# Attention over eight batches, with the loop on the engines written out as straight code

## The reference, cut to what matters

```python
x: (8, 512, 128) float32;  H = 16 heads of DH = 64
mod = silu(c) @ wmod                      # six rows per batch: sa, ca, ga, sb, cb, gb
h = layernorm(x) * (1 + ca) + sa
q, k, v = h @ Wq.T, h @ Wk.T, h @ Wv.T    # per head
q, k = l2norm(q) * q_scale, l2norm(k) * k_scale
attn = softmax(q @ k.T * DH ** -0.5)
x = x + ga * ((attn @ v) @ Wo.T + bo)
h = layernorm(x) * (1 + cb) + sb
x = x + gb * (shared_ffn(h) + top2_of_8_experts(h))   # experts with a capacity limit
```

## Time and profile before

| what | value |
|---|---|
| median of 3 runs | 1329.26 us (1327.91 to 1329.69) |
| profiled execution, its own time | 1331.88 us |
| its span, first to last instruction | 1330.0 us |
| mean granted TensorE clock | 0.967 |
| TensorE matmul busy | 1244.9 us, 94% of the span |
| VectorE, ScalarE, GpSimd busy | 988.1, 972.8, 849.6 us |
| attention batches 1 to 6 (the loop) | 157.5 to 894.6 us |

### The profile page before, as it was taken

One profiled execution on the slowest core, in us unless ns is written; L12 is line 12 of the kernel. 1 busy time (PEld: TensorE's weight loads), 2 busy tenths in 40 slices (PEclk: granted clock), 3 DMA queues, 4 the chain that ended last, 5 costly groups with the idle time before them and its releaser, 6 DMA issues. The chain is left out here.

```text
span 1330.0 us, 31765 instructions
## 1 busy us (share of the span) xinstructions
PE 1244.9 (94%) x9690; PEld 823.8 (62%) x9690; DVE 988.1 (74%) x1995; ACT 972.8 (73%) x2077; POOL 849.6 (64%) x1679
## 2 busy tenths in 40 slices
PE   4899999999999999999999999999997578999997
PEld 4556666656665665666566656666653455788886
DVE  3678778877877887788778778877874675576676
ACT  4677778777877776887678777877874556688886
POOL 2667677667866776776667766767764756344443
PEclk8799999999999999999999999999999689899999
DMA  5000000000000000000000000000002000544442
GB/s 139 2 1 2 1 2 2 2 4 1 2 3 3 2 2 4 2 2 2 4 1 2 2 4 2 1 2 1 2 1 77 6 1 5 109 100 108 101 101 51
DMA packets 36669, 28.58 MB, mean 21 GB/s; under 512 B 8832, under 2 KB 34688, under 8 KB 36480
## 3 DMA queue, kind: packets, MB, share of 16 engines
q1 hardware_dynamic: 35296, 25.92, 8.5%
q10 hardware_dynamic: 1184, 0.40, 0.1%
HBM read 24.09 MB, written 2.23 MB: 20 GB/s over the span
## 5 line engine op out<-in xcount | busy, mean ns | idle before, releaser
L714 ACT ACTIVATE probs<-bank,neg_max 128x512 f32<-128x512 f32 x512 | 347.7, 684 | 223.0 <-DVE neg_max L836 213.7
L836 DVE TENSOR_REDUCE neg_max<-bank 128x1 f32<-128x512 f32 x512 | 329.3, 685 | 143.2 <-PE bank L533 141.5
L573 PE MATMUL bank<-probsT,qkv 128*64 128x512 f32 x1024 | 275.6, 617 | 0.9 <-DVE oT L853 0.9
L533 PE MATMUL bank<-operands 64*128 64x512 f32 x1536 | 249.8, 430 | 1.8 <-ACT probs L714 0.7
L549 PEld LDWEIGHTS T<-ident,probs 64*128 64x128 f32 x4096 | 168.6, 139 | 47.5 <-issue 22.1
L503 PEld LDWEIGHTS bank<-operands,hT_h 128*128 128x128 f32 x254 | 48.2, 190 | 209.8 <-issue 207.0
L549 PE MATMUL T<-ident,probs 64*128 64x64 f32 x4096 | 171.8, 223 | 4.0 <-issue 3.0
L533 PEld LDWEIGHTS bank<-operands 64*128 64x128 f32 x1536 | 125.8, 186 | 64.2 <-issue 40.3
L987 POOL TENSOR_TENSOR sq<-qkv 128x256 f32<-128x256 f32 x252 | 150.1, 615 | 12.1 <-ACT qkv L693 12.0
L842 DVE COPY probsT<-T 128x1024 f32<-128x1024 f32 x128 | 155.3, 1213 | 0.2
L1691 POOL TENSOR_TENSOR hid_l<-act_out,hid_h 128x512 fp32r<-128x512 f32 x64 | 82.8, 1294 | 111.8 <-ACT hid_h L1593 111.8
(11 more groups left out here) (254 smaller groups left out, 2397.7 us busy)
## 6 DMA issues: line engine op xcount, KB each, us to landing
probsT<-gate_scratch SPq DMA_DIRECT2D x64, 256.0 KB, 4.7
out<-x_all SPq DMA_DIRECT2D x8, 256.0 KB, 4.6
probsT<-in_L_ffn_fc_w SPq DMA_DIRECT2D x1, 1024.0 KB, 10.2
raw<-in_L_attn_Wq SPq DMA_DIRECT2D x1, 512.0 KB, 4.2
raw<-in_L_attn_Wk SPq DMA_DIRECT2D x1, 512.0 KB, 7.4
raw<-in_L_attn_Wv SPq DMA_DIRECT2D x1, 512.0 KB, 8.6
raw_o<-in_L_attn_Wo SPq DMA_DIRECT2D x1, 512.0 KB, 8.7
probsT<-in_L_ffn_sh_w SPq DMA_DIRECT2D x2, 256.0 KB, 2.9
```

The costliest lines, as they stand in the source:

```text
L533: last = nc.tensor.matmul(s_bank(hp, 2 * pair + head)[:], own[rows, q, toks], own[rows, k], start=((q, k) == (QH, KH)), stop=(q == QL))
L573: last = nc.tensor.matmul(O_BANK[rows, :], qkv[:, hp % 4, j, cols], probsT[:, hp % 2, head, j], start=(j == 0), stop=(j == NT - 1), skip_g ...
L714: nc.scalar.activation(probs[:, i % 4], s_bank(hp, i)[:], ACT.Exp, bias=neg_max[:, i:i + 1], accum_out=row_sum[:, hp % 2, i:i + 1]).then_i ...
L836: nc.vector.reduce_max(neg_max[:, i:i + 1], s_bank(hp, i)[:], AX.X, negate=True).then_inc(max_done, 1)
```

## The change

The loop over batches 1 to 6 goes, on TensorE, ScalarE, VectorE and GpSimd alike, and b is a Python number in all eight. No matmul, copy or transfer is added or taken away, and none changes its place among the others.

```diff
             def over_batches(engine, batch):
 
-                batch(0)
-                with engine.Fori(1, LAST) as b:
+                for b in range(B):
                     batch(b)
-                batch(LAST)
```

## The result

The straight program takes 1318.89 us (median of 4 runs, 1318.27 to 1319.43) where the kernel before takes 1328.59 (4 runs): a ratio of 0.9926, 95% interval 0.9909 to 0.9943. On another chip the comparison was made again (the run again_after): 1318.02 against 1329.83, ratio 0.9908, interval 0.9892 to 0.9925. The profiled execution took 1318.57 us, its span 1316.6.

A forecast was written before the change was run, and what follows sets the result against it. TensorE, busy 94% of the span, was taken to set the attention's pace. Savings of 13.3 us (turns) plus 0.5 (registers), 13.8 off the profiled 1331.88, gave 1318.1, and 1316.2 us for the runs, range 1312.5 to 1320.

The forecast's parts named there:

- the clock's rival: Slow-clock stretches at about 1.3 us each, two or three more in attention or router's stage: 1319 to 1320; chance 8 in 100.
- The turn, on the path: TensorE's turn between attention batches costs 2.07 + 0.41 = 2.48 us; five turns make 12.4 us to be saved.
- the check by whole passes: Batches 1 to 6 took 737.1 us against six passes without turns, 723.8: 13.3 us saved in the profiled execution.
- clean pass: An attention loop pass without any turn, put at 122.7 - 2.07 = 120.63 us.
- The second part is ScalarE and VectorE starting again behind TensorE: The turn's later 0.41 us, in the next pair at a batch's start, laid to these engines restarting.
- The other engines' turns, hidden: VectorE's, ScalarE's and GpSimd's turns fall within TensorE's standstill; VectorE's 7.3 us over five goes too, so nothing shows.
- I take 0.5 saved: Attention batches 1 to 6: constants replace register waits and arithmetic, 1.0 us at most over six; 0.5 us taken as saved.
- Added code at nothing: Straight attention code needs about one 16 KB instruction block in 14 us, asked for ahead; costed at nothing.
- The first rival: TensorE stalls at straight attention code's 51 instruction blocks; a 2.48 us stall every third block gives 1357; chance 4 in 100.
- The second: Rival: TensorE's standstill between attention batches has another cause and returns, only register work saved: 1328.8 us; chance 3 in 100.
- The third: Rival: the experts' loop moves to a worse place, six turns of 2.48 us cost 14.9: 1331.1 us; chance 3 in 100.
- the one fall of the clock: Behind the attention's fifth turn the granted clock was 0.50 for 3.3 us, some 1.3 us, counted to the turn.

The follow-up runs named there:

- again_after: The straight kernel, unedited, run again beside the kernel before on another chip: 1318.02 against 1329.83 us, ratio 0.9908.
- The loop of two batches: Kernel before with two batches in each loop pass on all four engines, three passes and two turns: 1322.78 us, ratio 0.9938.
- The short loop: Against the kernel before, TensorE alone loops and batches 1 to 6 turn a quarter of the probabilities, body 1,567 instructions: 1299.10 us; straight twin 1298.51.
- the loops of one pass: Kernel before with its loop over batches 1 to 6 made six loops of one pass each: 1316.21 us, ratio 0.9911.
- the body of 1,823: Against the kernel before, TensorE alone loops and batches 1 to 6 turn half of the probabilities (`tiles` 2): 1312.52 us, one run.
- the body of 2,079: Against the kernel before, TensorE alone loops and batches 1 to 6 turn three quarters of the probabilities (`tiles` 3): 1330.47 us, one run.

## Why the prediction came out as it did

The forecast was 1316.2 us in 1312.5 to 1320; measured were 1318.89 and, on the other chip, 1318.02. Both lie in the range, 2.7 and 1.8 us above the forecast. (By its own chances the forecast and the clock's rival have 0.90, not the 0.91 from which it takes a little off.)

*The turn, on the path: right, and a little too dear.* The pair at a batch's end went from 6.67 to 4.60 us, as read from the one place where the loop was left without a turn. But the 2.48 us were read at one turn, and turns differ: nine without a fall of the clock cost 2.0 to 2.6, 2.3 in the mean, so five cost 11.3 (by the stretches without a fall) and not 12.4. For the profiled execution, fall included, the check by whole passes gave 13.3 us against 12.9 measured; the 0.4 are its clean pass, 120.63 us, which came out at 120.70. Against its own profiled execution the sum gave 1318.1 us; it took 1318.57.

*"The second part is ScalarE and VectorE starting again behind TensorE": wrong in its cause.* What stands behind the first pair is in part the other engines' own turns. It is not the same each time: in the nine turns it is 0.01 to 0.43 us, 0.3 in the mean, and in the three with TensorE alone looping 0.0 to 0.13. With TensorE straight and only the others looping, 0.4 of it stays in the pair behind the turn and the rest comes later in the pass, 1.0 us in all. *"The other engines' turns, hidden"* was therefore true only in part: of about 1.0 us each, 0.4 showed (2.3 us a turn against 1.9 with TensorE alone). The list of waits had said that they stand there to be laid open, with 7.3 us at L847 in 5 pieces. How the 0.4 divides among VectorE, ScalarE and GpSimd was not tried.

*"I take 0.5 saved" for the registers: mis-sized, it is nothing.* From scores of head pair 3 to scores of head pair 6 in batch 6 the straight kernel takes 851.13 - 805.50 = 45.63 us, against 45.56 before:

```profile
805.50 0.98 PE L531 MATMUL bank<-operands 64*128 64x512 f32 x6
...
851.13 0.96 PE L531 MATMUL bank<-operands 64*128 64x512 f32 x6
```

Step by step in that stretch there are gains of 0.1 us and losses of 0.1 to 0.2 at other places; the sum is nil. The loop of two batches shows it with registers on all four engines: its passes that don't end in a turn take 120.6 to 120.7 us, as in straight code. The short loop has 705.6 us with registers on TensorE and 706.2 without, but TensorE has 32 us of idle time there.

*Added code at nothing: right.* The first rival, stalls at the blocks of straight code, is refuted: the largest "issue" piece on TensorE's matmuls between 60 and 1000 us is 0.7 us. The second (the turn's time has another cause) is refuted by the 4.60 us between batches 1 and 2 of the straight kernel. The third (the experts' loop in a worse place) did not come: its branch still has a median of 208 ns, and writing it out changes nothing.

```profile
L1486 PEldq COMPARE_BRANCH  x7: 76/208/230, 1166.1 to 1302.5; - x7
```

*The clock: the other mis-sized term.* I counted the one fall of the clock into the saving of the profiled execution and gave it half weight for the timed runs. The two executions of the kernel before that I have traces of differ in just this: batches 1 to 6 take 737.1 us with a fall and 735.3 without. The saving in that stretch is 12.9 us (against 724.2) or 11.3 (against 724.0) accordingly; the two comparisons of medians gave 9.7 and 11.8.

Most of what is left goes with the granted clock outside the attention's middle, for which I had no term. It differs from execution to execution. Here are the first 60 us and the part behind 1000 us, the straight kernel first, then the loops of one pass:

```profile
0.00:60.00 60.00, 38.41 (x217) 29.82 (x217) 30.63 (x93) 30.03 (x66) 23.74 (x84) 0.77 0.32 78
1000.00:1316.60 316.60, 270.79 (x1166) 208.81 (x1164) 203.14 (x491) 224.14 (x374) 157.72 (x141) 0.91 0.31 69
...
0.00:60.00 60.00, 36.74 (x217) 28.50 (x217) 30.60 (x93) 30.21 (x69) 24.48 (x84) 0.83 0.32 78
1000.00:1314.00 314.00, 266.68 (x1164) 205.93 (x1164) 203.55 (x490) 224.02 (x374) 156.66 (x140) 0.93 0.29 70
```

The middles are alike (724.2 and 724.4 us), and the two executions took 1318.57 and 1315.79. Single runs show the same by their mean clock. At 0.968 the kernel before has five of its 53 runs with a recorded clock, 1330.3 to 1332.4, median 1331.4; the straight kernel has five, 1318.3 to 1319.4, median 1318.8: 12.6 us apart. (The mean holds the falls behind turns too, which are part of the saving.) The four straight runs of the first comparison stood at 0.968 to 0.969. Those that they were set against have no clock on record, but other runs with times like theirs, 1327.84 to 1329.69 us, stood at 0.969 to 0.975. So the forecast took its saving from runs with the faster clock, and that is the likely reason why it came out too low; it is worked out from the runs and was not tested.

The rule of the Trainium skill that I weighed against the trace ("Advanced Engine Details and Errata", section Control Flow Timing, about 108 ns for a compare-and-branch) is near a branch that is not taken (67 to 83 ns) and misses one that is taken over a long body by a factor of thirty. Another of its pages fits better: "Runtime: NRT & Kernel Launch", section Instruction fetch mechanics, says that a taken branch whose target is no longer held makes the sequencer wait for a transfer, and the q8 packet 1 us after each such branch agrees. The same section speaks of a window of two pages of 256 instructions; that doesn't hold for TensorE here, where 1,567 instructions went round with no packet on q8. It also gives TensorE room for 2048 instructions; here a body of 1,823 was already too long.

## What to carry to other kernels

Look for "issue" pieces whose count is the number of a loop's turns, and read the branch's own duration by the loop's line: on TensorE a long body pays per turn, a short one pays nothing, so fewer turns, a shorter body or straight code all work, and writing out a short loop gains nothing. The packets on the engine's instruction queue tell which of the two a loop is. On the other engines the branch's row stays short, and only the wait behind it shows the price. Take a loop away on all engines at once: TensorE alone gave 6.3 us of about 11, and the other three alone nothing that could be measured, because TensorE's turn covered most of theirs. The first and last pass of a loop, and batches written out beside it, tell beforehand what the passes would take without turns.

## What the runs showed that I had not expected

**The clock falls behind a turn.** In the middle of the attention the granted clock fell to 0.50 only right behind one of TensorE's turns over a long body: once in the kernel before, twice with TensorE's loop alone, once with the body of 1,823 and behind all five turns with the body of 2,079. The stretches of that last one, the first ahead of the first fall:

```profile
60.00:278.00 218.00, 213.33 (x1787) 129.84 (x1787) 174.45 (x320) 166.89 (x381) 155.40 (x328) 1.00 0.01 2
...
278.80:282.00 3.20, 3.20 (x18) 2.02 (x16) 0.83 (x2) 0.00 (x0) 2.50 (x10) 0.50 0.00 0
401.60:404.80 3.20, 3.20 (x10) 2.10 (x10) 0.75 (x1) 0.48 (x1) 2.34 (x12) 0.50 0.00 0
524.50:527.70 3.20, 3.20 (x11) 2.09 (x11) 0.61 (x1) 0.49 (x1) 2.37 (x11) 0.50 0.01 3
647.40:650.60 3.20, 3.20 (x9) 2.22 (x7) 0.00 (x0) 0.49 (x1) 2.35 (x11) 0.50 0.02 5
770.30:773.50 3.20, 3.20 (x8) 2.74 (x9) 0.37 (x3) 0.49 (x1) 2.01 (x10) 0.50 0.03 5
```

Each begins within two microseconds of the end of the turn and takes TensorE to 1.2 GHz; VectorE and ScalarE are busy for under 0.9 us in each. None of the traces without such turns has one there. That is nine falls behind the 27 long turns of the six traces that have them, so a pause of 2 us is not enough by itself; why five in five in one execution and none in another was not settled. It is part of why that kernel, with a quarter less of L549, took 1330.47 us, above the kernel before: its five turns cost 3.4 to 3.8 us each, where turns of TensorE alone without a fall cost 1.9 in the mean.

**The bound on a body.** A branch over 1,567 instructions took 0.2 us and one over 1,823 took 3.3, while the page of the Trainium skill named above has room for 2048. The same page's blocks of 256 instructions may reconcile the two, by an estimate: 1,823 instructions need eight blocks, 2048 are eight, and q8 moved nine packets a pass, one more than the body needs. If that ninth, asked for ahead from behind the body's end, takes the first one's place, the start is gone when the branch comes. The counts fit it (ten packets for 2,079 instructions, eleven for 2,335, and 1,567 with the block ahead come to eight), but it was not tested, nor where between 1,567 and 1,823 the bound lies. For the other engines the runs bound it only between the experts' loop, where no wait at a turn shows, and the attention's (on VectorE 352 instructions), where one does.
